# Redistributing the products for the row maxima over the steps of an attention loop

## Chip, cores and metric

One NeuronCore of a Trainium2 chip. The metric is the device time of one execution of the whole kernel in microseconds, the median over several runs.

## What is computed

A transformer layer on x of shape (2, 1024, 256) in float32, cut here to what matters:

```python
x = x + attention(rigid_transform(x))      # 16 heads of 16, causal, softmax over 1024 keys
x = x + moe_ffn(laplacian_reaction(x))     # 8 experts, top 2, hidden 1024
# attention, per batch and head:
scores = einsum('bhqd,bhkd->bhqk', Q, K) / sqrt(16), masked causally
A = softmax(scores)                        # needs the maximum of each row
Z = einsum('bhqk,bhkd->bhqd', A, V)
```

The rigid transform is a bilinear gather, the FFN routes each row to two of eight experts.

## The kernel before, in words

The kernel runs three stages: the rigid transform (about the first 200 us, with the second batch's transform going on later beside the attention), the attention (about 260 to 646 us), and the experts (a loop over 39 tiles, to the end). The change lies in the attention.

**Groups and steps.** The 32 (batch, head) pairs are done four heads at a time, in 2 * NG = 8 groups, numbered n = 0 to 7 (0 to 3 are the first batch, 4 to 7 the second). A group has NS = 12 steps; step s takes one block of 128 keys against one half (512) of the queries: `STEPS` (line 64) lists (half, key block), steps 0 to 7 for half 1, steps 8 to 11 for half 0. The causal mask cuts the width of a step to 512, 128, 512, 256, 512, 384, 512, 512 columns in steps 0 to 7 and 512, 128, 384, 256 in steps 8 to 11. In each step TensorE makes four scores (one per head, keys on the partitions; lines 1354 and, for the mask on the diagonal, 1359), ScalarE turns each into exponentials (line 1095), and TensorE adds the weighted values of the step before (`weighted`, line 1340). Scores go round three PSUM banks, so score t waits for exponential t - 3.

**Maxima.** The exponential subtracts the row maximum. That comes in as three more rows of the query operand of the score product, so the maxima of group m must be known before its first score. They are computed ahead, in earlier groups: for each head and each of 12 row pieces r, TensorE makes the scores again with queries on the partitions (`chunk`, lines 1169 and, on the diagonal, 1175), and VectorE reduces them (line 1734). A **pair** `(p, r)` is the two heads 2p and 2p + 1 at piece r: two products into two neighbouring banks and one reduction of both. Pieces have different numbers of keys (`chunk_of`, line 550): r = 0 and 5 have 128; 1 and 7 have 256; 2 and 9 have 384; 3, 4, 6, 8, 10 and 11 have 512. Each group needs 24 pairs.

After the last pair of a group, `(1, 11)`, VectorE takes the larger of two parts and negates it (`negate`, lines 1700 and 1701). Then TensorE turns the 32 columns into rows (`turn_max`, line 1279, which waits for the negation), VectorE splits the rows into three bf16 parts (lines 1743 to 1750), and the SP queue stores them into the operand stack (line 632). TensorE waits for these stores before the first score of the group.

**Side uses and their places.** Everything that TensorE does beside scores and weighted values is a "side use": a pair, the turn of the maxima, a sum over heads (`sum`), turns of the second batch's warped rows (`turn_w`), its projections (`project`, `values`), and, from group 4 on, the output of the first batch (`turn_z`, `attend`), the Laplacian (`lap`) and the router (`turn_du`, `logits`, `rank`). `attention_plan` (line 473) writes for each group and step the list of side uses. All sides share two sets of two PSUM banks in turn, so a side use waits until the use before the last has been read. VectorE reads them in the same order. In a step TensorE runs: score 0, the first side use of the list, scores 1 and 2, the weighted values of the step before, the second side use, score 3, and then all further side uses (lines 1368 to 1382).

**Where the pairs stand before.** `LATE_PAIRS` puts 16 pairs, two a step, into steps 0 to 7 of the group before (n computes those of n + 1), and `EARLY_PAIRS` the other eight, two a step, into steps 8 to 11 of the group before that (n computes those of n + 2). The early ones are pieces 7, 0, 1 and 5. In groups 0 and 4 nothing was done before, so there each of steps 0 to 7 has three pairs for n + 1 (one early, then two late), and steps 8 to 11 have two early ones for n + 2. Group 3 computes the maxima of group 4, whose operands come late: there `ALL_PAIRS` is laid three a step into steps 3 to 10, turn_max in step 11 (lines 495 to 498). Group 7 has no pairs. So the pairs per group are 32, 24, 16, 24, 32, 24, 16, 0, in all 168.

**The second batch's warp beside groups 0 to 2.** GpSimd gathers taps (lines 855 and 859) and mixes them (`mix`, lines 881 to 890) for eight blocks; ScalarE makes their weights (`hat`, lines 1003 to 1009) at places in its order of steps given by `HATS_AT` (line 81): the weights of block 5 begin at group 0, step 10, those of block 6 at group 1, step 2, those of block 7 at group 1, step 8. The first of them waits for the gather of its fractions. The projections of the second batch's queries and keys are in steps 8 to 11 of group 2 and steps 0 and 1 of group 3.

Of the kernel before, what the change touches and what calls it, by code (L numbers as in the profile page):

```python
# [54 lines left out]
NG = H // HG  # L55
# [19 lines left out]
EARLY_PAIRS = {8: [(0, 7), (1, 7)], 9: [(0, 0), (1, 0)], 10: [(0, 1), (1, 1)], 11: [(0, 5), (1, 5)]}  # L75
LATE_PAIRS = {0: [(0, 4), (1, 4)], 1: [(0, 2), (1, 2)], 2: [(0, 6), (1, 6)], 3: [(0, 9), (1, 9)],
              4: [(0, 8), (1, 8)], 5: [(0, 3), (1, 3)], 6: [(0, 10), (1, 10)], 7: [(0, 11), (1, 11)]}
LAST_PAIR = (1, 11)
ALL_PAIRS = [(pair, r) for r in (0, 7, 1, 5, 4, 2, 6, 9, 8, 3, 10, 11) for pair in range(2)]
# [87 lines left out]
def build(nc, x, shift, angle, zx, zy, zr, wq, bq, wk, bk, wv, bv, wo, bo, wr, br, w1, b1, w2, b2, consts, out):  # L167
    ctx = ExitStack()
    with ctx:
# [101 lines left out]
        for u in range(2):  # L271
            at = 2 * BAND + 2 * 3 * R * P + u * (9 * J - (J - D))
# [200 lines left out]
        def attention_plan():  # L473

            plan = [[[] for _ in STEPS] for _ in range(2 * NG)]
            late = NG - 1
            for n in range(2 * NG):
                at = plan[n]
                for s in range(NS):
                    if n in (0, NG) and s in LATE_PAIRS:  # L480
                        early = [pair for t in sorted(EARLY_PAIRS) for pair in EARLY_PAIRS[t]]
                        at[s] += [("pair", early[s], n + 1)] + [("pair", p, n + 1) for p in LATE_PAIRS[s]]
                    elif n + 1 < 2 * NG and n != late and s in LATE_PAIRS:
                        at[s] += [("pair", p, n + 1) for p in LATE_PAIRS[s]]
                    elif n + 2 < 2 * NG and n not in (late - 1, late) and s in EARLY_PAIRS:
                        at[s] += [("pair", p, n + 2) for p in EARLY_PAIRS[s]]
                if n + 1 < 2 * NG and n != late:
                    at[TURN_STEP].append(("turn_max", 0, n + 1))
            for k, (n, s) in enumerate(TURN_AT):
                plan[n][s].append(("turn_w", k, 1))  # L490
            for j, (n, s) in enumerate(PROJECT_AT):
                plan[n][s].append(("project", j, 1))
            for j, (n, s) in enumerate(VALUES_AT):
                plan[n][s].append(("values", j, 1))
            n, first = FIRST_OF_NEXT
            for k, pair in enumerate(ALL_PAIRS):
                plan[n][first + k // 3].append(("pair", (pair[0], pair[1]), n + 1))
            plan[n][NS - 1].append(("turn_max", 0, n + 1))
            for n in range(2 * NG):
                at = plan[n]  # L500
                at[10].insert(0, ("sum", 1, n))
                if n:
                    at[2].insert(0, ("sum", 0, n - 1))
                if n == NG:
                    for i, s in ((1, 3), (0, 4)):
                        at[s].append(("turn_z", i, 0))
                    for i, s in zip(ROW_ORDER, (5, 6, 7, 8)):
                        at[s].append(("attend", i, 0))
                if n == NG + 1:
                    for (what, i), s in zip(ROUTE_PLAN[0:3], (9, 10, 11)):  # L510
                        at[s].append((what, i, 0))
                if n == NG + 2:
                    at[0].append((*ROUTE_PLAN[3], 0))
                    for (what, i), s in zip(ROUTE_PLAN[4:12], (4, 6, 8, 9, 9, 10, 10, 11)):
                        at[s].append((what, i, 0))
                    at[11].append(("turn_b1", 0, 1))
                if n == NG + 3:
                    at[1].append((*ROUTE_PLAN[12], 0))
                    at[11].append(("turn_z", 1, 1))
            return plan  # L520

        ATTENTION = attention_plan()
        FIRST_USE = CHUNKS + 1
        LAST_USES = FIRST_USE + sum(len(uses) for at in ATTENTION for uses in at)
# [1442 lines left out]
```

## Time and profile before

| | |
|---|---|
| median of 3 runs | 1048.71 us (1047.28 to 1050.87) |
| the profiled execution | 1051.46 us, span 1049.6 us |
| mean granted TensorE clock | 0.849 of full |
| busy over the span | TensorE 71%, VectorE 48%, ScalarE 34%, GpSimd 29% |
| attention's first score, last weighted values | 260.0 us, 646.4 us |
| pairs of maxima: reductions | 168 |

In the rows, PE is TensorE's matmuls and PEld its weight loads, DVE is VectorE, ACT ScalarE, POOL GpSimd, SPq the SP engine's DMA queue. A row of the timeline has start, duration, engine, line, operation and operands; in square brackets stands how long the engine was idle before it, and what it waited for. A row of windows has the stretch, its length, the busy time of each engine with the number of instructions, the granted clock, the share of the DMA engines and GB/s. The first score of a step (line 1354) marks where the step begins.

### The profile page before, as it was taken

The numbers are of one execution on the slowest core, as the hardware profiler recorded it, in microseconds if no ns is written. First come the engines' busy times: TensorE is split into PE (matmuls) and PEld (weight loads), VectorE is DVE, ScalarE is ACT, GpSimd is POOL, SyncE is SP. The second block draws the span as 40 slices with busy tenths as digits, with TensorE's granted clock in tenths as the row PEclk, the third lists the DMA queues.
The fourth block names the chain that finished last, engine by engine and source line by source line (L and its number), as shares of the span: only waits on it lengthen the run. The fifth ranks groups of instructions, "written<-read, shape, count | busy, mean of one in ns | idle before, by whom it ended". The sixth has DMA issues, their size and how long they took to land.

```text
span 1049.6 us, 14316 instructions
## 1 busy us (share of the span) xinstructions
PE 745.2 (71%) x4027; PEld 446.0 (42%) x4028; DVE 501.7 (48%) x1039; ACT 361.3 (34%) x912; POOL 308.8 (29%) x292
## 2 busy tenths in 40 slices
PE   0351111852787787978999967708999999999992
PEld 0340111421332332533446423604766776676672
DVE  6173556573565771577688632622332323333230
ACT  0122333343465553444574553001223223222320
POOL 0113444165898732200200042150112111211211
PEclk9855555865898898999999996758999999999996
DMA  7688787799352306959722063641221221222123
GB/s 254 210 260 319 267 299 233 235 266 281 122 180 102 100 2 179 335 153 341 253 81 82 2 224 124 215 161 24 33 35 30 35 35 31 33 33 35 30 30 90
DMA packets 95523, 150.99 MB, mean 144 GB/s; under 512 B 9365, under 2 KB 69322, under 8 KB 95306
## 3 DMA queue, kind: packets, MB, share of 16 engines
q1 hardware_dynamic: 74136, 85.76, 26.2%
q0 software_dynamic: 16784, 61.51, 20.0%
q10 hardware_dynamic: 4546, 3.08, 1.0%
q8 instruction: 21, 0.34, 0.1%
q14 instruction: 36, 0.29, 0.1%
HBM read 95.86 MB, written 56.37 MB: 145 GB/s over the span
## 4 chain that ended last, share of the span: by engine, by line
PE 54%; DVE 12%; DMA 12%; POOL 8%; issue 7%; ACT 3%; SPq 2%; another core or an unknown queue 0%; POOLq 0%; ACTq 0%; DVEq 0%
PE psum L1399 13%; PE psum L1415 13%; PE psum L1340 6%; PE psum L1354 4%; PE psum L1169 4%; DMA arena<-table,tap_col 4%; DVE arena L1734 3%; PE psum L1407 3%; PE psum L1182 2%; PE psum L1303 2%; DMA arena<-table,tap_index 2%; SPq L569 2%; DMA table<-arena 2%; POOL arena L881 1%; DMA qk_rows<-arena 1%
## 5 line engine op out<-in xcount | busy, mean ns | idle before, releaser
L1095 ACT ACTIVATE arena<-psum 128x512 f32<-128x512 f32 (+3 forms) x384 | 171.0, 491 | 167.2 <-PE psum L1359 119.5
L1734 DVE TENSOR_REDUCE arena<-psum 128x2 f32<-128x1024 f32 (+3 forms) x168 | 155.1, 954 | 86.4 <-PE psum L1175 62.4
L1150 ACT ACTIVATE arena<-psum,b_cols 128x128 f32<-128x128 f32 x312 | 84.9, 383 | 263.9 <-PE psum L1407 263.9
L1354 PE MATMUL psum<-arena 99*128 99x512 bf16 (+3 forms) x384 | 117.0, 347 | 50.1 <-ACT arena L1095 20.6
L1415 PE MATMUL psum<-arena 128*128 x624 | 142.9, 382 | 3.1 <-ACT arena L1150 3.1
L1399 PE MATMUL psum<-arena 128*128 x312 | 143.3, 603 | 0.8 <-DVE arena L1908 0.7
L966 POOL DMA_INDIRECT results<-arena,home x39 | 60.7, 1557 | 271.2 <-DVE arena L1927 203.8
L1169 PE MATMUL psum<-arena 96*128 96x512 bf16 (+4 forms) x384 | 111.8, 361 | 25.6 <-DVE arena L1734 11.5
L1415 PEld LDWEIGHTS psum<-arena 128*128 128x128 f32 x624 | 116.8, 192 | 18.4 <-issue 3.8
L1916 DVE COPY arena<-psum 128x1024 f32<-128x1024 f32 x39 | 47.7, 1224 | 98.8 <-PE psum L1399 98.8
L1340 PE MATMUL psum<-arena 128*32 128x512 f32 (+3 forms) x768 | 88.2, 534 | 1.1 <-POOL arena L849 0.6
L1399 PEld LDWEIGHTS psum<-arena 128*128 128x128 f32 x312 | 57.3, 194 | 59.0 <-issue 59.0
L1169 PEld LDWEIGHTS psum<-arena 96*128 96x128 bf16 (+1 forms) x384 | 36.9, 105 | 100.5 <-DVE arena L1734 44.7
L1354 PEld LDWEIGHTS psum<-arena 99*128 99x128 bf16 x384 | 38.8, 103 | 95.6 <-ACT arena L1095 41.2
L1210 PE MATMUL psum<-cst,arena 128*128 128x128 f32 (+1 forms) x180 | 37.5, 397 | 54.3 <-DMA arena<-padded,band_col 48.3
L1923 DVE TENSOR_TENSOR arena<-psum,arena 128x256 f32<-128x256 f32 x39 | 16.5, 424 | 117.0 <-PE psum L1415 114.1
L1219 PE MATMUL psum<-cst,arena 128*128 128x128 f32 x16 | 5.5, 447 | 90.2 <-DVE arena L1666 90.2
L1210 PEld LDWEIGHTS psum<-cst,arena 128*128 128x128 f32 (+1 forms) x180 | 33.4, 203 | 57.4 <-issue 42.3
L1359 PE MATMUL psum<-mask_kq,ident_b 128*128 128x128 bf16 x256 | 57.2, 231 | 0.0
L1175 PE MATMUL psum<-mask_qk,ident_b 128*128 128x128 bf16 x256 | 56.5, 237 | 0.0
L947 POOL DMA_INDIRECT pairs_x<-warped_words,x_index x32 | 31.1, 972 | 82.2 <-DVEq L1845 73.1
L1219 PEld LDWEIGHTS psum<-cst,arena 128*128 128x128 f32 x16 | 2.3, 204 | 93.1 <-issue 93.1
(207 smaller groups left out, 998.9 us busy)
## 6 DMA issues: line engine op xcount, KB each, us to landing
pairs_x<-zeros SPq DMA_DIRECT2D x4, 4160.0 KB, 23.8
arena<-L_ffn_W SPq DMA_DIRECT2D x16, 1024.0 KB
arena<-qk_rows SPq DMA_DIRECT2D x16, 768.0 KB, 12.1
table<-arena SPq DMA_DIRECT2D x20, 384.0 KB
qk_rows<-arena SPq DMA_DIRECT2D x16, 384.0 KB, 4.7
arena<-pairs_x SPq DMA_DIRECT2D x39, 130.0 KB, 2.1
qk_rows<-arena SPq DMA_DIRECT2D x16, 256.0 KB, 4.7
padded<-arena SPq DMA_DIRECT2D x2, 1328.0 KB
```

The source lines that it names most:

```text
L966: g_.indirect_dma_start(results, bass.IndirectOffsetOnAxis(ap=home[:, t:t + 1], axis=0), y_tile, None, compute_op=ALU.add).then_inc(y_stor ...
L1095: nc.scalar.activation(probs[at % 2][h][:, q0:512], banks[turn % SCORE_BANKS][:, q0:512], ACT.Exp, scale=DH ** -0.5).then_inc(exp_done, 1)
L1150: ins = nc.scalar.activation(hidden_t[:, f], banks[3 + f // 4][:, (f % 4) * P:(f % 4 + 1) * P], ACT.Relu, bias=b1_cols[:, bass.ds(e, 1), f])
L1169: ins = t_.matmul(bank[:, 0:keys], stacks[0:KROWS, bass.ds(g, 1), 0, head, qb * P:(qb + 1) * P].squeeze(1).squeeze(1), stacks[0:KROWS, bas ...
L1175: ins = t_.matmul(bank[:, at_:at_ + P], ident_b[:], mask_qk[:], start=False, stop=True)
L1210: ins = t_.transpose(banks[g][0:w, r * P:(r + 1) * P], band[u][:, at_:at_ + w], ident)
L1340: ins = t_.matmul(banks[OUT_BANK][32 * h:32 * h + 32, q0:512], v_group[:, n % 2, kt, h], probs[at % 2][h][:, q0:512], start=first, stop=last)
L1354: ins = t_.matmul(bank[:, q0 - half * 512:512], stacks[0:KROWS + 3, g, 1, h, kt * P:(kt + 1) * P], stacks[0:KROWS + 3, g, 0, h, q0:(half + ...
L1359: ins = t_.matmul(bank[:, at_:at_ + P], ident_b[:], mask_kq[:], start=False, stop=True)
L1399: ins = t_.matmul(banks[half], x_t[:, c], w1_all[:, bass.ds(e, 1), c, half * 512:(half + 1) * 512].squeeze(1), start=c == 0, stop=c == DC - 1)
L1415: ins = t_.matmul(banks[5][:, 0:D], hidden_t[:, f], w2_all[:, bass.ds(e, 1), f].squeeze(1), start=f == 0, stop=f == FC - 1)
L1734: v.reduce_max(part[:, 2 * pair:2 * pair + 2, qb], psum[:, at:at + 2, 0:keys], AX_X).then_inc(max_read, 1)
```

## The change

`attention_plan` places the pairs of the next group otherwise. In every group but 3 and 7, steps 0 to 7 get three consecutive entries of `ALL_PAIRS` each, all for n + 1; steps 8 to 11 get none. The order of the pieces in `ALL_PAIRS`, both pairs of each in turn, is 0, 7, 1, 5, 4, 2, 6, 9, 8, 3, 10, 11. So by keys the steps hold: step 0 (128, 128, 256), step 1 (256, 256, 256), step 2 (128, 128, 512), step 3 (512, 384, 384), step 4 (512, 512, 384), step 5 (384, 512, 512), steps 6 and 7 (512, 512, 512). Pairs per group are then 24 in groups 0 to 6 and 0 in group 7. Group 3 is placed by the lines that stay. Where pairs leave a list, what stands behind them in it moves to an earlier place of the step: the turn of the maxima in step 8 becomes the first side use.

```diff
@@ -477,13 +477,8 @@
             for n in range(2 * NG):
                 at = plan[n]
                 for s in range(NS):
-                    if n in (0, NG) and s in LATE_PAIRS:
-                        early = [pair for t in sorted(EARLY_PAIRS) for pair in EARLY_PAIRS[t]]
-                        at[s] += [("pair", early[s], n + 1)] + [("pair", p, n + 1) for p in LATE_PAIRS[s]]
-                    elif n + 1 < 2 * NG and n != late and s in LATE_PAIRS:
-                        at[s] += [("pair", p, n + 1) for p in LATE_PAIRS[s]]
-                    elif n + 2 < 2 * NG and n not in (late - 1, late) and s in EARLY_PAIRS:
-                        at[s] += [("pair", p, n + 2) for p in EARLY_PAIRS[s]]
+                    if n + 1 < 2 * NG and n != late and s in LATE_PAIRS:
+                        at[s] += [("pair", p, n + 1) for p in ALL_PAIRS[3 * s:3 * s + 3]]
                 if n + 1 < 2 * NG and n != late:
                     at[TURN_STEP].append(("turn_max", 0, n + 1))
```

## Rows read from the trace of the kernel before

**Rows 1.** The page: the chain that ended last, by engine.

```profile
PE 54%; DVE 12%; DMA 12%; POOL 8%; issue 7%; ACT 3%; SPq 2%; another core or an unknown queue 0%; POOLq 0%; ACTq 0%; DVEq 0%
```

**Rows 2.** Windows: group 5 in three stretches, 4 in two, 2 and 6 (steps 4-7).

```profile
522.02:533.42 11.40, 10.52 (x86) 4.75 (x85) 9.28 (x12) 8.77 (x20) 0.67 (x1) 1.00 0.47 185
533.42:544.86 11.44, 11.44 (x82) 4.38 (x81) 9.24 (x9) 8.41 (x17) 0.00 (x0) 1.00 0.00 0
544.86:563.12 18.26, 17.44 (x137) 11.85 (x136) 13.71 (x28) 7.43 (x18) 0.00 (x0) 1.00 0.02 4
...
488.80:510.31 21.51, 18.82 (x114) 8.04 (x112) 14.55 (x17) 8.63 (x16) 2.80 (x6) 0.92 1.06 370
510.31:522.02 11.71, 10.95 (x106) 6.14 (x106) 8.07 (x21) 6.83 (x16) 2.78 (x6) 1.00 0.56 186
...
377.45:388.89 11.44, 11.44 (x82) 4.44 (x81) 9.24 (x9) 7.93 (x16) 0.84 (x2) 1.00 0.00 1
...
576.44:589.93 13.49, 12.66 (x90) 5.30 (x89) 10.61 (x11) 8.15 (x16) 0.00 (x0) 1.00 0.01 1
```

**Rows 3.** Lines by form, VectorE, 252 to 660 us: the reductions of the pairs.

```profile
L1734 DVE TENSOR_REDUCE arena<-psum 128x2 f32<-128x1024 f32 x84 | 100.1, 1221 | 36.6 <-PE psum L1169 20.5 <-PE psum L1175 16.1
L1734 DVE TENSOR_REDUCE arena<-psum 128x2 f32<-128x768 f32 x28 | 26.2, 954 | 12.8 <-PE psum L1175 12.8
L1734 DVE TENSOR_REDUCE arena<-psum 128x2 f32<-128x512 f32 x28 | 18.7, 687 | 27.6 <-PE psum L1175 24.7 <-remote 2.3
L1734 DVE TENSOR_REDUCE arena<-psum 128x2 f32<-128x256 f32 x28 | 11.7, 421 | 9.4 <-PE psum L1175 8.8 <-issue 0.2 <-DVE x L1773 0.2
```

**Rows 4.** Timeline: ScalarE at the start of step 2 of group 1.

```profile
325.30 0.53 ACT L1003 ACTIVATE x<-late_frac,row_bias 128x256 f32<-128x256 f32 x1 [6.15 <-DMA late_frac<-fracs,frac_index]
```

**Rows 5.** Windows: steps 7, 8 and 9 of group 3.

```profile
448.55:452.36 3.81, 3.70 (x27) 1.41 (x26) 3.02 (x4) 2.29 (x5) 0.00 (x0) 1.00 1.06 375
452.36:456.37 4.01, 3.69 (x27) 1.40 (x26) 2.94 (x4) 2.86 (x6) 0.00 (x0) 1.00 1.08 245
456.37:460.14 3.77, 3.27 (x28) 1.44 (x26) 3.33 (x4) 1.27 (x5) 0.00 (x0) 1.00 0.79 161
```

**Rows 6.** Timeline, TensorE in group 5: two small pairs and what follows each.

```profile
550.01 0.23 PE L1169 MATMUL psum<-arena 96*128 96x128 bf16 x1
...
550.25 0.22 PE L1354 MATMUL psum<-arena 99*128 99x128 bf16 x1
...
554.14 0.28 PE L1169 MATMUL psum<-arena 96*128 96x256 bf16 x1
...
554.49 0.33 PE L1354 MATMUL psum<-arena 99*128 99x384 bf16 x1
```

**Rows 7.** Timeline: turn of the maxima in group 5, negation and turn in group 6.

```profile
547.77 0.27 PE L1279 MATMUL psum<-cst,arena 128*32 128x128 f32 x1
...
591.12 0.19 DVE L1700 TENSOR_TENSOR arena<-arena 128x32 f32<-128x32 f32 x1
...
591.67 0.27 PE L1279 MATMUL psum<-cst,arena 128*32 128x128 f32 x1 [1.30 <-DVE arena L1701]
```

**Rows 8.** Timeline: the same in group 1, beside GpSimd's mixing of block 6.

```profile
346.31 3.08 DVE L1700 TENSOR_TENSOR arena<-arena 128x32 f32<-128x32 f32 x1
347.54 1.80 POOL L881 TENSOR_TENSOR arena<-arena,x 128x768 f32<-128x768 f32 x1
...
349.43 1.83 DVE L1701 TENSOR_SCALAR arena<-arena 128x32 f32<-128x32 f32 x1
...
351.91 0.28 PE L1279 MATMUL psum<-cst,arena 128*32 128x128 f32 x1 [3.71 <-DVE arena L1734]
...
355.87 0.72 POOL L890 TENSOR_TENSOR x<-x 128x256 f32<-128x256 f32 x1
```

**Rows 9.** Timeline: the SP queue's stores of maxima, and group 3's first score.

```profile
410.15 1.95 SPq L632 DMA_DIRECT2D arena<-arena  x3
...
413.46 0.58 PE L1354 MATMUL psum<-arena 99*128 99x512 bf16 x1 [7.80 <-issue]
```

## The prediction

> **What bounds the kernel now.** I read the page first: the chain that ended last is mostly TensorE (54%), with VectorE 12%, and the attention loop lies in the middle of it [rows 1]. So I cut the loop where its steps begin. The windows [rows 2] show stretches of the last three groups that matter: steps 0 to 7 of group 5 are 11.40 + 11.44 = 22.8 us long, steps 8 to 11 are 18.26 us; in group 4 the last four take 11.71 us. In steps 4 to 7 of group 5 TensorE is busy all 11.44 us, VectorE 9.24, ScalarE 8.41. All three are near full there: a full-width step holds four exponentials and two or three pairs, and no engine has much room. A pair of maxima is two products on TensorE, then one reduction on VectorE that must free the two banks before the pair after next. The reductions cost 0.42, 0.69, 0.95 and 1.22 us for 128, 256, 384 and 512 keys [rows 3].
>
> The first groups are different. In step 2 of group 1 ScalarE sat idle 6.15 us, until the fractions of the late gather landed at 325.30 [rows 4]. That gather is issued behind GpSimd's mixing, so group 0 and the first two steps of group 1 end when GpSimd lets them.
>
> **What the change moves.** The number of pairs stays 168, and no instruction is added or taken away. The eight small pairs (row blocks 7, 0, 1, 5: 256, 128, 256 and 128 keys, twice each) leave steps 8 to 11 of groups 0, 1, 4 and 5, and are done one group later for groups 1 and 5, in steps 0 to 7 of groups 1, 2, 5 and 6. Groups 0 and 4 already have three pairs in steps 0 to 7, but spread them as one small and two large; now the small ones come first and the large ones last. Group 3 and group 7 keep their lists. Loads of the stacks are needed later, never earlier, so no DMA moves onto the path.
>
> VectorE's bill for steps 4 to 7 now is eight reductions of 1.22 us, 9.8 us. After it is (1.22 + 1.22 + 0.95) twice and 3 x 1.22 twice, 14.1 us. Steps 0 to 3 hold 8.7 us now and 8.8 us after, for the small ones lie there: I cost these steps at nothing, covered by TensorE and ScalarE as now. (Were that cover gone, they would pay at most the 2.4 us of TensorE below.)
>
> **What three pairs cost in a step.** The kernel shows this already. In group 3 the same order starts at step 3, so its steps 7, 8 and 9 do exactly the sets (6,6,9), (9,8,8) and (3,3,10). They took 3.81, 4.01 and 3.77 us [rows 5], 11.59 us for 3.40 + 3.40 + 3.66 = 10.46 us of reductions, a factor 1.108. So steps 4 to 7 take 14.1 x 1.108 = 15.6 us where they took 11.44: **+4.2 us**. The bounds: TensorE's issue time of the moved pairs alone from below, 2.4 us; a full 4.0 us for every step of steps 2 to 7 from above, about +7. I take 4.2, since those rows are the same instructions.
>
> **What leaving gives back.** A small pair holds TensorE for 0.24 us (550.01 to 550.25, 128 keys) or 0.35 us (554.14 to 554.49, 256 keys) [rows 6], so eight are 4 x 0.24 + 4 x 0.35 = 2.4 us. Their reductions are 4.4 us, but VectorE has room there. I take 2.4 (bounds 0, where ScalarE's exponentials cover them, and 4.4).
>
> **A wait that comes in their place.** Step 8 is [pair, pair, turn of the maxima] now, and [turn] after. The turn waits for the negated maxima, which wait for the last reduction. In group 5 two pairs stand between, and the turn starts without a wait; in group 6, which has no early pairs, TensorE waited 1.30 us [rows 7]. Behind it in TensorE's queue are scores 1 to 3 of step 8, and ScalarE waits for these. Groups 4 and 5 gain this wait: +1.3 each. In groups 2 and 6 the last large pair now stands after score 3, nearer the turn: +0.5 each (bounds 0 and 1.2, one more reduction).
>
> **Group by group.**
> - Group 0: 0. It loses eight pairs, and the 6.15 us of idle time only grow.
> - Group 1, from 325.3: +4.2 in steps 4 to 7. But see what waits at its end [rows 8]: the first of the two negations, 0.19 us in group 6 [rows 7], took 3.08 us at 346.31, and the second 1.83 us, beside GpSimd's mixing; TensorE waited 3.71 us. The mixing ends at 355.87 + 0.72 = 356.6, and steps 2 to 7 don't move that. Started 4.2 us later, the negations still lie in the mixing, and the chain behind them ends with it, as now. Then the pairs of steps 9 to 11 are gone, and what is left over of the 4.2 us I set against these. Sum **0** (bounds -4 and +4).
> - Group 2: +4.2 + 0.5 = **+4.7**. Its end is passed on: group 3 starts at 413.46, after the SP queue's stores of maxima at 410.15 [rows 9]; these stand behind its stores of parts, which hang on the projections in steps 8 to 11 of group 2.
> - Group 4: steps 4 to 7 hold 14.1 instead of 12.1 us of reductions (+2.0), steps 0 to 3 hold 8.8 instead of 10.8; the late steps also carry the attention outputs and take 21.51 us now, so I give +2.2 and -1.5. Steps 8 to 11: -2.4 + 1.3. **-0.4**.
> - Group 5: +4.2 - 2.4 + 1.3 = **+3.1**.
> - Group 6: two more copies of 0.69 us are in steps 4 to 7: (14.1 + 1.4) x 1.108 = 17.2, against 13.49: +3.7, and 0.5: **+4.2**.
> - Group 7 and all that follows: moved as a whole, for the expert loop waits for scattered pairs, which wait for the attention's last rows.
>
> Sum: 0 + 4.7 - 0.4 + 3.1 + 4.2 = **+11.6 us**. The profiled execution took 1051.46 us (its span 1049.6), 2.8 above the median of the three runs; 1051.5 + 11.6 = 1063.1 for it, and 1048.7 + 11.6 = **1060.3** by the median.
>
> One place where a rule bears on this: at 346.31 a VectorE operation of 0.19 us took 3.08 us; a GpSimd operation began inside it at 347.54, and it ended, at 349.39, only with that one's end, 349.34 [rows 7, 8]. The Trainium skill, SBUF — State Buffer, Who interferes with whom, says that an operation of VectorE with two SBUF inputs and one of GpSimd exclude each other, whoever issues first. By that rule the negations, coming 4.2 us later, might slip in front of a GpSimd operation and be over in one wait, and group 1 would give back up to 3 us, for 1057.3 us in all; the trace shows the first of them losing to an operation that began after it, so the sum keeps 0.
>
> **Rivals.**
> 1. **The third pair fits into idle time** (the other side, faster). Place: steps 4 to 7 of groups 1, 2, 5 and 6. For it: VectorE is idle 2.2 of 11.44 us there. Then those steps cost 0, and 2.4 us come back in each of groups 1, 4 and 5: -7.2, 1041.5 us. It decides if a step of three large pairs takes no longer than one of two, 11.44 / 4 = 2.9 us. Against it: group 3's steps [rows 5], and TensorE's 11.44 of 11.44 us [rows 2]. Chance 0.07.
> 2. **Only TensorE's issue time counts**: +2.4 in place of 4.2 or 3.7 in groups 2, 5 and 6, the rest as above: 2.9 - 0.4 + 1.3 + 2.9 = +6.7, 1055.4 us. Chance 0.13. With group 1 also giving back 4 us: +2.7, 1051.4, no difference that could be told. Chance 0.08.
> 3. **The mixing hits group 1 harder**, or new idle time lowers the granted clock (the 21.51 us of group 4 were at 0.92, the other stretches at 1.00). Another +4 in group 1, and 0.08 of the 48 us (15.6 + 15.6 + 17.2) of steps 4 to 7 of groups 2, 5 and 6 added, +4: 1068. Chance 0.10.
> 4. **The change doesn't do what it says.** It can't in group 3 and 7, which keep their lists, and in group 0, where a wait takes all; this is in the sum. That nothing moves in the others I exclude by the lists.
>
> **Chances.** The forecast (1056 to 1066) 0.62; the rivals 0.07, 0.13, 0.08 and 0.10. The range from 1051 to 1068 leaves out rival 1, half of the "no difference" case and the upper half of rival 3, 0.16 in all. A change under 0.3% (3.1 us) can hardly be told from none here. Faster 0.08, within 0.08, slower 0.84.
>
> **What would show it.** Steps 4 to 7 of groups 2 and 5 at 15 to 16 us, of group 6 near 17; VectorE busy over 90% of them; the idle time at 325.3 longer and its end unmoved; the turn of the maxima in group 5 waiting over a microsecond; steps 8 to 11 of group 5 about 1 us shorter; group 1 ending near 365 as now. It is wrong if steps 4 to 7 stay under 13 us, or if group 1 ends more than 4 us off.

## The result, and the profile after

The changed kernel took 1063.09 us (median of 4 runs, 1058.27 to 1065.95), the kernel before 1047.99 us on the same occasions. The ratio is 1.0135, with a 95% interval of 1.009 to 1.018: slower by 14 us (15.1 between the two medians), where +11.6 us and 1060.3 us were forecast. The profiled execution took 1064.55 us, with a span of 1062.7 us. Lines in the changed kernel carry numbers lower by 5 from the edit on: its reductions of pairs are L1729, its scores L1349, the turn of the maxima L1274.

The page has the same number of instructions and nearly the same chain as before [rows 1].

```profile
span 1062.7 us, 14316 instructions
...
PE 55%; DVE 12%; DMA 11%; POOL 8%; issue 7%; SPq 3%; ACT 2%; another core or an unknown queue 0%; POOLq 0%; ACTq 0%; DVEq 0%
```

So the number of instructions is the same, and the time went into waits between them and into a lower granted clock. Windows of the changed kernel show where: group 1 from its gate (the weights of block 6), then groups 2 to 7. The columns are the stretch, its length, the busy time of PE, PEld, DVE, ACT and POOL, the granted clock, the DMA share and GB/s.

```profile
322.11:363.15 41.04, 34.48 (x198) 13.75 (x199) 24.65 (x30) 24.65 (x56) 30.12 (x23) 0.74 0.33 119
363.15:421.77 58.62, 45.09 (x286) 19.25 (x286) 31.48 (x45) 25.56 (x56) 19.59 (x18) 0.88 0.17 55
421.77:480.10 58.33, 49.33 (x313) 24.22 (x314) 33.53 (x51) 25.16 (x54) 7.68 (x9) 0.94 0.85 245
480.10:526.96 46.86, 42.95 (x289) 19.25 (x290) 31.35 (x45) 22.75 (x49) 6.36 (x13) 0.90 0.99 333
526.96:572.73 45.77, 41.79 (x301) 21.88 (x300) 32.73 (x48) 25.07 (x54) 0.67 (x1) 0.96 0.13 47
572.73:618.41 45.68, 40.93 (x326) 21.78 (x325) 32.96 (x55) 22.85 (x50) 0.67 (x1) 1.00 0.12 48
618.41:660.44 42.03, 29.84 (x203) 10.16 (x201) 10.20 (x43) 22.25 (x52) 15.61 (x16) 0.80 0.43 151
```

The same stretches before were 39.61, 48.55, 59.08, 49.48, 41.10, 40.41 and 42.89 us long; group 2 of them, at a clock of 0.94:

```profile
364.91:413.46 48.55, 37.52 (x255) 15.84 (x254) 26.99 (x38) 24.68 (x55) 18.62 (x18) 0.94 0.20 67
```

The differences are +1.4, +10.1, -0.8, -2.6, +4.7, +5.3 and -0.9, together +17.2. In this execution the gate itself came 3.2 us earlier (322.11 against 325.30), with 7.25 us of idle time before it:

```profile
322.11 0.52 ACT L998 ACTIVATE x<-late_frac,row_bias 128x256 f32<-128x256 f32 x1 [7.25 <-DMA late_frac<-fracs,frac_index]
```

And the experts took 0.9 less. 17.2 - 3.2 - 0.9 = 13.1, the difference of the two spans. Why the gate was earlier stays open. It may not be chance: the five profiles of kernels with three pairs in each of steps 0 to 7 of groups 1 and 2 (the changed kernel, first_batch, narrow, turn_9, spread) have it at 320.6 to 323.6 us, the eight others at 323.6 to 328.2, and already the attention's first score came at 257.1 to 258.9 in the five and at 258.2 to 263.8 in the others.

Inside the groups, the windows that answer to [rows 2] and to its group 5 first: steps 0 to 3, 4 to 7 and 8 to 11 of group 5; then steps 4 to 7 and 8 to 11 of group 4, steps 4 to 7 of group 2, steps 4 to 7 of group 6.

```profile
527.00:538.90 11.90, 11.29 (x106) 5.90 (x105) 8.41 (x15) 9.09 (x21) 0.67 (x1) 1.00 0.47 178
538.90:554.28 15.38, 13.89 (x94) 5.26 (x93) 13.10 (x13) 9.17 (x18) 0.00 (x0) 1.00 0.00 0
554.28:572.73 18.45, 16.57 (x105) 10.68 (x104) 11.22 (x22) 6.80 (x17) 0.00 (x0) 0.91 0.01 2
...
495.70:517.17 21.47, 19.46 (x110) 7.79 (x107) 16.74 (x17) 8.69 (x16) 2.80 (x6) 0.92 1.06 363
517.17:526.96 9.79, 8.93 (x74) 3.93 (x74) 5.06 (x14) 6.44 (x16) 2.89 (x6) 1.00 0.77 259
...
379.61:395.09 15.48, 14.21 (x94) 5.46 (x93) 12.78 (x13) 8.39 (x16) 0.00 (x0) 0.97 0.00 1
586.87:604.24 17.37, 15.18 (x102) 6.07 (x101) 14.47 (x15) 8.58 (x17) 0.00 (x0) 1.00 0.00 1
```

Steps 4 to 7 took 15.38, 15.48 and 17.37 us; 15.6, 15.6 and 17.2 were forecast. VectorE is busy 13.10 of 15.38 us, 85%, where it was 9.24 of 11.44; TensorE, busy all 11.44 us before, now has 1.5 us of gaps. But steps 8 to 11 of group 5 took 18.45 us, no less than the 18.26 with the eight pairs in them. Their first step shows why; the timeline of the changed kernel at the turn of the maxima, in group 2 and in group 5:

```profile
397.40 0.27 PE L1274 MATMUL psum<-cst,arena 128*32 128x128 f32 x1 [1.88 <-DVE arena L1696]
...
398.19 1.13 ACT L1090 ACTIVATE arena<-psum 128x512 f32<-128x512 f32 x2 [1.97 <-PE psum L1354]
...
398.56 0.20 PEld L1335 LDWEIGHTS psum<-arena 128*32 128x32 f32 x8 [0.52 <-issue]
398.56 1.94 PE L1335 MATMUL psum<-arena 128*32 128x512 f32 x8
...
556.60 0.27 PE L1274 MATMUL psum<-cst,arena 128*32 128x128 f32 x1 [1.88 <-DVE arena L1696]
```

TensorE waits 1.88 us for the second negation, against none in group 5 and 1.30 in group 6 before [rows 7], and in group 2 ScalarE waits 1.97 us behind it. Then the weighted values (L1335) there take 1.94 us instead of 1.07: the granted clock has fallen to half. The windows of step 8 of groups 5, 6 and 2 (4.77, 5.25, 8.42 us), and of steps 0 to 3 of group 2, show it at 0.90, 1.00, 0.80 and 0.82:

```profile
554.28:559.05 4.77, 2.89 (x19) 0.88 (x18) 4.08 (x11) 2.38 (x5) 0.00 (x0) 0.90 0.01 3
604.24:609.49 5.25, 3.37 (x27) 1.71 (x26) 3.46 (x10) 2.58 (x5) 0.00 (x0) 1.00 0.00 0
395.09:403.51 8.42, 6.25 (x25) 2.13 (x24) 3.79 (x10) 2.03 (x4) 0.00 (x0) 0.80 0.00 0
363.15:379.61 16.46, 14.18 (x106) 6.94 (x107) 10.09 (x16) 7.75 (x19) 12.51 (x10) 0.82 0.01 2
```

Step 8 of group 5 before, with its two pairs in front of the turn:

```profile
544.86:547.88 3.02, 3.02 (x27) 1.42 (x26) 2.30 (x5) 2.66 (x5) 0.00 (x0) 1.00 0.03 5
```

In group 4, where TensorE makes an output of the first batch between the last pair and step 8, the turn waits for next to nothing:

```profile
517.78 0.27 PE L1274 MATMUL psum<-cst,arena 128*32 128x128 f32 x1 [0.16 <-DVE arena L1696]
```

### The profile page after: what moved, and what is told of

It is laid out like the page before. It is cut to its first block, busy times and chain, and to the rows that moved or that the text cites. A ratio compares the mean times of both kernels' runs of the same rounds, so it can differ in the third digit from the quotient of the medians.

```text
span 1062.7 us, 14316 instructions
## 1 busy us (share of the span) xinstructions
PE 758.5 (71%) x4027; PEld 448.4 (42%) x4028; DVE 502.1 (47%) x1039; ACT 363.3 (34%) x912; POOL 310.7 (29%) x292
## 3 DMA queue, kind: packets, MB, share of 16 engines
q10 hardware_dynamic: 4546, 3.08, 1.0%
## 4 chain that ended last, share of the span: by engine, by line
PE 55%; DVE 12%; DMA 11%; POOL 8%; issue 7%; SPq 3%; ACT 2%; another core or an unknown queue 0%; POOLq 0%; ACTq 0%; DVEq 0%
PE psum L1394 13%; PE psum L1410 13%; PE psum L1335 6%; DVE arena L1729 5%; PE psum L1164 4%; PE psum L1349 4%; PE psum L1402 3%; DMA arena<-table,tap_col 2%; DMA table<-arena 2%; PE psum L1177 2%; PE psum L1298 2%; SPq L564 2%; DMA arena<-table,tap_index 2%; POOL arena L817 1%; POOL arena L876 1%
## 5 line engine op out<-in xcount | busy, mean ns | idle before, releaser
L1090 ACT ACTIVATE arena<-psum 128x512 f32<-128x512 f32 (+3 forms) x384 | 173.4, 491 | 181.4 <-PE psum L1354 128.2
L1729 DVE TENSOR_REDUCE arena<-psum 128x2 f32<-128x1024 f32 (+3 forms) x168 | 154.1, 954 | 83.9 <-PE psum L1170 66.7
L1349 PE MATMUL psum<-arena 99*128 99x512 bf16 (+3 forms) x384 | 122.3, 353 | 46.6 <-ACT arena L1090 20.3
L1164 PE MATMUL psum<-arena 96*128 96x512 bf16 (+4 forms) x384 | 114.3, 368 | 26.8 <-DVE arena L1729 13.6
L1335 PE MATMUL psum<-arena 128*32 128x512 f32 (+3 forms) x768 | 93.3, 560 | 0.8 <-ACT arena L1090 0.8
L1349 PEld LDWEIGHTS psum<-arena 99*128 99x128 bf16 x384 | 39.4, 105 | 102.2 <-ACT arena L1090 47.6
L1205 PE MATMUL psum<-cst,arena 128*128 128x128 f32 (+1 forms) x180 | 36.1, 386 | 54.5 <-DMA arena<-padded,band_col 48.5
L1214 PE MATMUL psum<-cst,arena 128*128 128x128 f32 x16 | 5.5, 445 | 88.7 <-DVE arena L1661 74.7
L1354 PE MATMUL psum<-mask_kq,ident_b 128*128 128x128 bf16 x256 | 58.3, 236 | 0.0
L1402 PE MATMUL psum<-cst,arena 128*128 128x128 f32 x312 | 40.5, 272 | 1.1 <-DVE arena L1911 1.1
```

The costliest lines, as they stand in the source:

```text
L1090: nc.scalar.activation(probs[at % 2][h][:, q0:512], banks[turn % SCORE_BANKS][:, q0:512], ACT.Exp, scale=DH ** -0.5).then_inc(exp_done, 1)
L1164: ins = t_.matmul(bank[:, 0:keys], stacks[0:KROWS, bass.ds(g, 1), 0, head, qb * P:(qb + 1) * P].squeeze(1).squeeze(1), stacks[0:KROWS, bas ...
L1205: ins = t_.transpose(banks[g][0:w, r * P:(r + 1) * P], band[u][:, at_:at_ + w], ident)
L1335: ins = t_.matmul(banks[OUT_BANK][32 * h:32 * h + 32, q0:512], v_group[:, n % 2, kt, h], probs[at % 2][h][:, q0:512], start=first, stop=last)
L1349: ins = t_.matmul(bank[:, q0 - half * 512:512], stacks[0:KROWS + 3, g, 1, h, kt * P:(kt + 1) * P], stacks[0:KROWS + 3, g, 0, h, q0:(half + ...
L1354: ins = t_.matmul(bank[:, at_:at_ + P], ident_b[:], mask_kq[:], start=False, stop=True)
```

## The experiments

The theory after this reading: a third pair costs each full-width step about a microsecond, half of it VectorE's; and the turn of the maxima, left alone in step 8, costs more than the small pairs that stood before it. The rivals: the loss is only bunching (the large pairs all at the end); it is made in one batch alone; or the wait is paid anyway, wherever the turn stands.

**The change in the first batch alone** (first_batch).

```diff
+                    if n < NG:
+                        if n != late and s in LATE_PAIRS:
+                            at[s] += [("pair", p, n + 1) for p in ALL_PAIRS[3 * s:3 * s + 3]]
-                    if n in (0, NG) and s in LATE_PAIRS:
+                    elif n in (0, NG) and s in LATE_PAIRS:
```

> The change in groups 0 to 2 alone; groups 4 to 6 as before. If the loss is made of the terms of the prediction as the profile of the changed kernel corrects them (group 1 +1.4, group 2 +10.1), it is 11 to 12 us of the 14 to 15, 1.011 of the time before; if each of groups 2, 5 and 6 pays the same 4.7 us, as was forecast, this kernel pays only 5 us (1.005). Group 2 should be 58 us long (48.6 before) with half clock near 374 to 381 and 398 to 401 us, groups 4 to 6 at 49, 41 and 40 us.

Measured: 1.0074 (1.0039 to 1.0108), 7.8 us, between the two expectations. Its profiled execution was the fastest of its ten (1049.85 us, the median is 1057.95), so it shows the change in groups 1 and 2 at its cheapest. Group 1 (from its gate), group 2, and of group 2 steps 0 to 3, 4 to 7 and 8:

```profile
321.60:359.15 37.55, 30.32 (x199) 12.16 (x199) 25.18 (x30) 24.15 (x56) 30.26 (x23) 0.87 0.37 130
359.15:413.64 54.49, 40.69 (x286) 17.95 (x286) 31.29 (x45) 25.46 (x56) 19.60 (x18) 0.97 0.18 60
...
359.15:373.10 13.95, 11.66 (x107) 6.21 (x107) 9.59 (x16) 7.52 (x19) 11.69 (x8) 1.00 0.01 2
373.10:388.48 15.38, 13.89 (x95) 5.25 (x93) 13.10 (x13) 8.58 (x17) 0.84 (x2) 1.00 0.00 1
388.48:395.38 6.90, 4.69 (x25) 1.78 (x24) 3.79 (x10) 1.98 (x4) 0.00 (x0) 1.00 0.00 0
```

These two groups run the same instructions as in the changed kernel (the same 286 matmuls in group 2), yet group 2 took 54.5 us at a granted clock of 0.97, not 58.6 at 0.88 (the expectation had 58). So some 4 of the 10.1 us there were the clock of one execution, and 5.9 us stay at the better clock: 1.4 in steps 0 to 3 (12.54 before), 3.9 in steps 4 to 7 (11.44) and 0.6 in step 8 (6.33). The fall of the clock in steps 0 to 3 isn't the change's alone: order_only, before_turn_9, late_early and turn_9_sparse below, whose lists in these steps are the old ones, have one there too.

**The change in the second batch alone** (second_batch).

```diff
+                    if n >= NG:
+                        if n + 1 < 2 * NG and s in LATE_PAIRS:
+                            at[s] += [("pair", p, n + 1) for p in ALL_PAIRS[3 * s:3 * s + 3]]
-                    if n in (0, NG) and s in LATE_PAIRS:
+                    elif n in (0, NG) and s in LATE_PAIRS:
```

> The change in groups 4 to 6 alone; groups 0 to 3 as before. first_batch lost 0.74%, 7.8 us. If the parts add up, this one loses the rest of the 1.35%, 6 to 7 us (1.006), with group 4 about 2 us shorter and groups 5 and 6 about 5 us longer each. If the loss comes from what the first batch's delay does later on, it is under 3 us.

Measured: 1.0080 (1.0056 to 1.0105), 8.4 us. With the other half that is 16 us for the whole's 14, within the intervals: the parts add up, and the loss is made in both batches. Group 5 took 44.1 us at full clock here, not 45.8, and its steps 8 to 11 16.82 us, not 18.45. Groups 5 and 6, and steps 8 to 11 of group 5:

```profile
519.66:563.76 44.10, 40.05 (x298) 20.90 (x299) 32.74 (x48) 24.97 (x54) 0.67 (x1) 1.00 0.13 49
563.76:609.48 45.72, 40.98 (x326) 21.81 (x325) 32.96 (x55) 22.88 (x50) 0.67 (x1) 1.00 0.14 48
...
547.01:563.83 16.82, 14.94 (x105) 9.73 (x104) 11.22 (x22) 6.70 (x17) 0.00 (x0) 1.00 0.01 2
```

**Narrow reductions, in the changed kernel and in the one before** (narrow, narrow_before).

```diff
-                    v.reduce_max(part[:, 2 * pair:2 * pair + 2, qb], psum[:, at:at + 2, 0:keys],
+                    v.reduce_max(part[:, 2 * pair:2 * pair + 2, qb], psum[:, at:at + 2, 0:P],
```

> The changed kernel with every reduction of a pair in groups 0 to 6 reading only its first 128 keys (0.42 us each instead of up to 1.22); all products stay. What is left out: the maxima over the other keys. If VectorE's reductions set the pace of the steps with three pairs, steps 4 to 7 of group 5 fall from 15.4 us to TensorE's own pace, about 12.5 to 13.5 us, and the kernel by 10 to 20 us, below the kernel before. If TensorE sets it, they stay at 15 us.

> The kernel before with the same narrowed reductions as in the run narrow (the maxima over all but the first 128 keys are left out). If two pairs a step are TensorE's business alone, steps 4 to 7 of group 5 stay near 11.4 us, and what the change costs with narrow reductions, 13.2 - 11.4 = 1.8 us a group, is TensorE's time for the moved pairs; the rest of the 3.9 us is VectorE's. Then it takes about 0.990. If VectorE sets the pace before as well, they fall under 10.5 us and the kernel to 0.980.

Measured: 0.9944 (0.9917 to 0.9971) and 0.9882 (0.9836 to 0.9929). With narrow reductions the change costs 0.0062, 6.5 us, not 14; by the two intervals this is anything from 1 to 12 us, so the windows say more than the totals. Steps 4 to 7 of group 5, first the changed kernel, then the one before:

```profile
524.23:537.44 13.21, 13.21 (x95) 5.49 (x94) 5.12 (x13) 9.07 (x18) 0.00 (x0) 1.00 0.00 0
```

```profile
524.06:535.50 11.44, 11.44 (x83) 4.39 (x82) 3.49 (x9) 8.41 (x17) 0.00 (x0) 1.00 0.00 0
```

Before the change the width of the reductions doesn't matter in these steps: 11.44 us with 9.24 us of VectorE's time or with 3.49, and TensorE busy throughout. With three pairs it does: 15.38 against 13.21. So of the 3.9 us that these steps gained in group 5, 1.8 us are TensorE's own time for the moved products, and 2.2 us come with the width of the reductions, VectorE's part. This is the largest term of the sum, now split.

**The turn of the maxima in step 9 of the changed kernel** (turn_9).

```diff
-TURN_STEP = 8
+TURN_STEP = 9
```

> The changed kernel with the turn of the maxima moved from step 8 to step 9 (first use there). If the wait for the negation is a cost of its own, step 8 of groups 2, 5 and 6 falls by 1.3 to 1.9 us and the kernel by 4 to 8 us against the changed one (1.007 of before); if the same time is only spent later, because step 8 hands its scores on at the pace of the reductions anyway, it is within 2 us of the changed kernel (1.013). If the maxima come too late for the next group, each group starts late and it is slower still.

Measured: 1.0042 (1.0020 to 1.0064), over 9 us less than the changed kernel's 1.0135, more than the 4 to 8 expected. Steps 4 to 7, 8, and 9 to 11 of group 5, and the turn there:

```profile
530.50:545.88 15.38, 13.89 (x94) 5.25 (x93) 13.10 (x13) 9.17 (x18) 0.00 (x0) 1.00 0.00 0
545.88:548.09 2.21, 2.21 (x18) 0.75 (x17) 2.10 (x4) 1.98 (x5) 0.00 (x0) 1.00 0.00 0
548.09:561.36 13.27, 12.78 (x89) 9.05 (x88) 9.12 (x18) 4.56 (x13) 0.00 (x0) 1.00 0.02 3
```

```profile
548.21 0.27 PE L1274 MATMUL psum<-cst,arena 128*32 128x128 f32 x1
```

Steps 4 to 7 are the same to the hundredth, step 8 takes 2.21 us instead of 4.77, and the turn waits for nothing. The clock stays full, also after it. Against first_batch and second_batch, whose steps 8 to 11 ran at the same clock in these groups, the move is worth 0.6, 1.3 and 1.2 us in groups 2, 5 and 6. From its gate group 1 took 35.54 us (41.04 in the changed kernel, 39.61 before), at 0.84 against 0.74; but group 1 varies: in four profiles that have it as it was before, that of the kernel before among them, it took 37.2 to 39.6 us.

The same move in the kernel before gains nothing (0.9998, below), though it takes away waits of 1.30 us in groups 2 and 6 there. So with the turn in step 9 the change costs 0.44% instead of 1.35%: some 9 of its 14 us, by the ratios, come only with the turn in step 8. That the wait itself makes up 3 us of this is shown by the windows; that the rest is the clock and group 1 is argued, from one execution each. No step of the forecast put more than 1.3 us on it at one place.

**The wait alone, in the kernel before** (turn_first).

```diff
-                    at[TURN_STEP].append(("turn_max", 0, n + 1))
+                    at[TURN_STEP].insert(0, ("turn_max", 0, n + 1))
```

> The kernel before with only the order in step 8 changed: the turn of the maxima first, the two small pairs behind it. This is the wait alone, without any pair moved to another group. If the wait costs 1.3 us in each group where pairs stood before the turn and no idle time covers it (1, 4 and 5), +4 us, 1.004; in group 1 it may cost nothing, for there the negation is late anyway: then +2.6. If it costs nothing, 1.000.

Measured: 1.0032 (1.0009 to 1.0055), 3.4 us. Step 8 of group 5 took 4.46 us where it took 3.02 before: +1.44 for a turn that stands before its two pairs instead of behind them. This fits the expectation of 1.3 us in each of groups 1, 4 and 5.

```profile
548.54:553.00 4.46, 3.16 (x28) 1.44 (x27) 3.21 (x9) 2.85 (x6) 0.00 (x0) 1.00 0.01 4
```

**The order alone** (order_only).

```diff
                     if n in (0, NG) and s in LATE_PAIRS:
-                        early = [pair for t in sorted(EARLY_PAIRS) for pair in EARLY_PAIRS[t]]
-                        at[s] += [("pair", early[s], n + 1)] + [("pair", p, n + 1) for p in LATE_PAIRS[s]]
+                        at[s] += [("pair", p, n + 1) for p in ALL_PAIRS[3 * s:3 * s + 3]]
```

> The kernel before, with only the order of the pairs in steps 0 to 7 of groups 0 and 4 changed to the new one; every pair stays in its group. By the prediction +0.7 us in group 4 and nothing in group 0: 1.001 or less, not to be told from 1. If bunching alone made the loss it would be over 1.003.

Measured: 0.9994 (0.9964 to 1.0024). The new order by itself costs nothing that can be told.

**The pairs spread evenly** (spread). The changed kernel with the old order of groups 0 and 4 in every group.

```diff
-                        at[s] += [("pair", p, n + 1) for p in ALL_PAIRS[3 * s:3 * s + 3]]
+                        early = [pair for t in sorted(EARLY_PAIRS) for pair in EARLY_PAIRS[t]]
+                        at[s] += [("pair", early[s], n + 1)] + [("pair", p, n + 1) for p in LATE_PAIRS[s]]
```

> The changed kernel with the same three pairs a step in steps 0 to 7, but each step one small and two large, the order that groups 0 and 4 had before. The reductions of steps 4 to 7 are then 12.1 us instead of 14.1, those of steps 0 to 3 10.8 instead of 8.8. If the loss comes from bunching the large ones in steps 4 to 7, where VectorE sets the pace, those steps take 13.5 us instead of 15.4 and steps 0 to 3 about a microsecond more: 1 us less in each of groups 1, 2, 5 and 6, 1.009 instead of 1.0135. If only the number of pairs in steps 0 to 7 counts, within 2 us of the changed kernel.

Measured: 1.0234 (1.0200 to 1.0267), slower than the changed kernel: both expectations missed. Steps 4 to 7 and 0 to 3 of group 5, and step 8 of group 6:

```profile
538.79:553.45 14.66, 13.28 (x99) 5.37 (x98) 10.97 (x13) 9.18 (x18) 0.00 (x0) 1.00 0.00 0
525.24:538.79 13.55, 12.05 (x102) 5.75 (x101) 10.26 (x15) 9.31 (x21) 0.67 (x1) 1.00 0.41 156
604.74:611.88 7.14, 5.27 (x27) 2.62 (x26) 3.54 (x10) 2.58 (x5) 0.00 (x0) 0.72 0.02 3
```

The late steps fell by 0.7 us, not 2, though VectorE's busy time in them fell by 2.1; the early ones grew by 1.6. So the loss isn't only bunching: three pairs in a step cost time even where VectorE is busy only 75% of it. And the clock fell again behind the turn's wait, in group 6 too (0.72). Why this order loses the clock more often than the other wasn't settled.

**Toward a faster kernel.** Three versions were tried; none beats the kernel before.

The turn in step 9, in the kernel before (before_turn_9):

```diff
-                    at[TURN_STEP].append(("turn_max", 0, n + 1))
+                    at[9].insert(0, ("turn_max", 0, n + 1))
```

> The kernel before with the turn of the maxima as the first use of step 9 instead of the last of the pairs' places in step 8; no pair moves. If the wait for the negation costs time wherever nothing stands before the turn, groups 2 and 6 gain 1.3 us or more each and group 1, where the negation is held up by GpSimd's mixing, up to 3: 0.995 to 0.998. If group 1's wait only moves to the next pair, which needs the same VectorE, only groups 2 and 6 gain: 0.998.

Measured: 0.9998 (0.9977 to 1.0020), no difference. Group 6 fell from 40.4 to 39.3 us in its profile, but in groups 4 and 5, where pairs stand in front of the turn, it had not waited before either, and groups 5 and 2 were 0.5 and 1.6 us longer.

The same with the early pairs behind it (late_early):

```diff
-EARLY_PAIRS = {8: [(0, 7), (1, 7)], 9: [(0, 0), (1, 0)], 10: [(0, 1), (1, 1)], 11: [(0, 5), (1, 5)]}
+EARLY_PAIRS = {9: [(0, 7), (1, 7), (0, 0)], 10: [(1, 0), (0, 1), (1, 1)], 11: [(0, 5), (1, 5)]}
```

> As before_turn_9, and the eight early pairs in steps 9, 10 and 11 (3, 3, 2) behind the turn, none in step 8, so that nothing stands between the negation and the scores of step 8. If emptying step 8 is what made group 1 shorter in turn_9 (35.5 us from its gate instead of 39.6), this kernel keeps that gain without the 4 us that groups 2, 5 and 6 pay for a third pair: 0.992 to 0.996, faster than both kernels. If steps 9 to 11 are too short for three pairs each, it is at 1.000.

Measured: 1.0064 (1.0032 to 1.0095), slower than either expectation. In group 5 steps 9 to 11 took 17.24 us, where the turn alone had made them 15.86 (before_turn_9), while step 8 took 2.57 after 2.91:

```profile
548.04:565.28 17.24, 15.77 (x122) 11.11 (x120) 12.29 (x25) 5.10 (x14) 0.00 (x0) 1.00 0.02 4
```

The turn waited for nothing there. So the small pairs cost little in step 8 and more in the narrower steps behind it.

The turn in step 9 in groups 2 and 6 only (turn_9_sparse):

```diff
+                    if n in (2, NG + 2):
+                        at[9].insert(0, ("turn_max", 0, n + 1))
+                    else:
+                        at[TURN_STEP].append(("turn_max", 0, n + 1))
```

> The kernel before with the turn of the maxima in step 9 in groups 2 and 6 only, where no pair stands between it and the negation. Group 6 took 1.1 us less so in before_turn_9, while groups 4 and 5 took 0.5 more. If these figures hold alone, 2 us less, 0.998, hardly to be told from 1; if the granted clock decides, anything from 0.996 to 1.002.

Measured: 0.9997 (0.9972 to 1.0022). What group 6 gives back is less than can be told.

## Why the prediction was right, and where it was off

- **Sign and size.** +11.6 us forecast, +14 us measured (1.0135); 1063.09 us lies in the range of 1051 to 1068. That the total came so near is in part luck: from group 1's gate to the end of the attention the two profiled executions differ by 17.2 us, not 11.6, and the total is nearer only because the gate came 3.2 us earlier and the experts took 0.9 less, neither of which the forecast had.
- **The terms at like clock.** Group 2 in the first_batch run, groups 5 and 6 in the second_batch run, against the kernel before, forecast and measured in us:

| | group 2 | group 5 | group 6 |
|---|---|---|---|
| steps 0 to 3 | 0, +1.4 | 0, +0.5 | 0, +0.8 |
| steps 4 to 7 | +4.2, +3.9 | +4.2, +3.9 | +3.7, +3.9 |
| steps 8 to 11 | +0.5, +0.6 | -1.1, -1.4 | +0.5, +0.6 |
| sum | +4.7, +5.9 | +3.1, +3.0 | +4.2, +5.3 |

- **What three pairs cost in steps 4 to 7** (+4.2, +4.2, +3.7): right. Measured +3.9 (15.38 - 11.44) in group 5, +4.0 in group 2, +3.9 in group 6. Group 3's steps [rows 5] were good rows to price it by, though not the same instructions throughout, as was said: the scores of its steps 7, 8 and 9 are 512, 512 and 128 columns wide, those of steps 4 to 7 are 512, 384, 512 and 512. VectorE was busy 83 to 85% of these steps, not over 90% as the signs had it. Its reason was half right: with narrow reductions 2.2 of group 5's 3.9 us go away, the rest is TensorE's. And it isn't a matter of VectorE's sum in those steps, as the factor 1.108 had it: by it the even spread would take 13.3 us there (8 x 1.22 + 2 x 0.69 + 2 x 0.42 = 12.0 us of reductions), and took 14.66.
- **Steps 0 to 3 at nothing**: this is the term that was put at nothing and wasn't, 2.7 us in three groups. They hold one more pair a step, and TensorE and ScalarE didn't cover it. In group 2 they went from 12.54 to 16.46 at a clock of 0.82, and to 13.95 at full clock in the first_batch run, so some 2.5 of the 3.9 us are the clock.
- **What leaving gives back and the wait in its place** (-2.4 + 1.3): right at full clock, and mis-sized where the clock falls. In the profiled execution steps 8 to 11 of group 5 gave back nothing (18.26 to 18.45), not 1.1. In the second_batch run, at full clock, they took 16.82 us and gave back 1.4, though the wait was 1.88 us there too, not 1.30. The 1.6 us between the two are the half clock behind the wait, for which the sum had no term. In group 4 the wait that was forecast didn't come (0.16 us). In groups 2 and 6 the +0.5 for the last large pair standing next to the turn fits 1.30 to 1.88. Moving the turn by one step won back over 9 us of the loss in all, of which 3 us are seen in groups 2, 5 and 6. The forecast had put 1.3 in groups 4 and 5 and 0.5 in groups 2 and 6, 3.6 us, and none in group 1.
- **Group 1 at 0** (bounds -4 and +4): +1.4 in the profile, -2.1 in the first_batch run (37.55 against 39.61), with the same instructions in it. Two executions of them differ by 3.5 us, so neither is told from 0. ScalarE was idle longer at the gate, 7.25 us after 6.15 [rows 4], as forecast; that the gate wouldn't move didn't hold (3.2 us earlier).
- **Group 2 at +4.7, passed on to group 3**: +5.9 at a clock of 0.97, +10.1 in the profiled execution. It was passed on in full: group 3 took 58.3 us after 59.1.
- **Group 4 at -0.4**: -2.6. Its steps 8 to 11 fell from 11.71 to 9.79, 1.9 us and not 1.1, for the turn didn't wait. Its steps 4 to 7, with more reductions in them, took 21.47 us after 21.51, where I had charged 2.2. But both executions had a stretch at half clock there (0.92). At full clock the old lists took 19.92 us in the first_batch run, so how much the reductions add isn't settled:

```profile
488.81:508.73 19.92, 17.22 (x114) 7.60 (x112) 14.55 (x17) 8.49 (x16) 2.80 (x6) 1.00 1.06 370
```

- **Groups 5 and 6 at +3.1 and +4.2**: +4.7 and +5.3; +3.0 and +5.3 at full clock.
- **Rivals.** The third pair wasn't free: those steps took 15.4 us, over the 13 named as the limit. TensorE's issue time alone would have given +6.7. The narrow runs give +6.5, but their interval is wide and they hold the waits too, so that this is so near is luck. Idle time lowering the granted clock, which I gave 0.10, is real in part: it is the 4 us between two executions of group 2, and 1.6 us in group 5. No difference, by group 1 giving back time, didn't come.
- **The port rule** (the Trainium skill, SBUF — State Buffer, Who interferes with whom) fits the first negation of group 1 in the changed kernel, and not the one before. In the changed kernel it took 0.97 us and ended with the GpSimd operation that was running, and the second then took its usual 0.18 us. Before they took 3.08 and 1.83 us, and the first ended only with a GpSimd operation that had begun 1.2 us after it [rows 8]. In the changed kernel the second was not held up, though the record of the next GpSimd operation starts 10 ns ahead of it, at 350.29; which of the two came first isn't shown:

```profile
348.41 1.80 POOL L880 TENSOR_TENSOR x<-x,arena 128x768 f32<-128x768 f32 x1
...
349.29 0.97 DVE L1695 TENSOR_TENSOR arena<-arena 128x32 f32<-128x32 f32 x1
350.29 1.85 POOL L881 TENSOR_TENSOR x<-x,arena 128x768 f32<-128x768 f32 x1
350.30 0.18 DVE L1696 TENSOR_SCALAR arena<-arena 128x32 f32<-128x32 f32 x1
```

The change isn't what made it short: two kernels with the old lists in group 1 have the same (1.51 and 0.18 us in order_only, 1.31 and 0.18 in turn_first). And the 3 us that were named didn't come back: the turn still waited 2.66 us, after 3.71, and group 1 took 1.4 us more, at a clock of 0.74 after 0.78.

## What to carry to other kernels

When background work is moved between stretches of a loop, price it where it lands by a stretch of the same kernel that already carries that load; that held here to 0.3 us in steps 4 to 7. Don't put the steps that look covered at nothing: one more pair in each of steps 0 to 3 cost 0.5 to 1.4 us a group. Then look at what stood in front of each wait that stays: two small pairs before a dependent one can be its cover. With them gone step 8 of group 5 grew by 1.3 us at full clock (3.02 to 4.35), though they had held TensorE for only 0.7 us. Moving the dependent operation one step later got that back here; in the kernel before, where the cover still stood in groups 4 and 5, the same move gained nothing.

## What was not expected of the hardware

A wait of under 2 us on TensorE can cost more than its length. In the changed kernel the granted clock fell to half (1.2 GHz) behind the 1.88 us wait at 397.4, and the eight weighted-value matmuls took 1.94 us for 1.07. It doesn't fall each time: the wait of 1.88 us before the turn stands nine times in the profiles of the changed kernel, spread, first_batch and second_batch (groups 2, 5 and 6), and the clock fell right behind it in five of them. Behind the nine waits of 1.30 us before a turn (the kernel before, order_only, turn_first, first_batch and second_batch) it never did. What decides it isn't shown. Between two runs the same group 2, with the same 286 matmuls, took 54.49 us at a mean granted clock of 0.97 and 58.62 us at 0.88. Where the wait was gone (the turn in step 9), there was no fall at that place in groups 2 and 5; but in first_batch and second_batch there was none either, with the wait.
